# Two expert passes of a routed layer: one loop over both passes, rows copied ahead, and an accumulating scatter into the output

## What is computed

```python
rh = relu(f @ router_w1 + router_b1)              # f = layernorm(x2)
top_w, top_i = top_k(softmax(rh @ router_w2 + router_b2), 2)
w = softmax(top_w)
h1 = relu(f @ expert_w1 + expert_b1)              # 6 experts, 256 x 256 each
h2 = relu(h1 @ expert_w2 + expert_b2)
out = x2 + sum over the two chosen e of w[e] * (h2 @ expert_w3 + expert_b3)[e]
```

## Time and profile before

| | us |
|---|---|
| median of three runs | 787.16 |
| the profiled execution, its own time | 785.95 |
| its span, first to last instruction | 783.9 |
| TensorE busy (matmul) | 677.8 |
| VectorE busy | 556.7 |
| ScalarE busy | 440.9 |
| GpSimd busy | 403.3 |

### The profile page before, as it was taken

The page is one execution under the profiler, slowest core; times in us unless marked ns, Lnnn a source line. Parts: engine busy times, 40 slices in busy tenths (PEclk is TensorE's granted clock), DMA queues, the critical chain, the costliest instruction groups (busy, mean ns, idle before and its releaser), DMA issues.

```text
span 783.9 us, 15402 instructions
## 1 busy us (share of the span) xinstructions
PE 677.8 (86%) x4705; PEld 621.5 (79%) x4705; DVE 556.7 (71%) x1423; ACT 440.9 (56%) x878; POOL 403.3 (51%) x446
## 2 busy tenths in 40 slices
PE   3877999999999888888860899999994799999992
PEld 2867788888888777777750799999993799999992
DVE  5674679888888867777864377777773477777772
ACT  2645566667777446767740465565651565656551
POOL 3465378876666100464444155556554155565553
PEclk9999999999999999989855699999998899999997
DMA  8885644544443454765144524444433534544420
GB/s 220 194 163 125 152 128 132 143 132 119 122 138 107 139 164 156 246 192 180 53 112 118 165 82 139 142 133 135 141 111 103 154 93 130 149 133 147 134 65 29
DMA packets 72463, 106.24 MB, mean 136 GB/s; under 512 B 24612, under 2 KB 45605, under 8 KB 72386
## 3 DMA queue, kind: packets, MB, share of 16 engines
q1 hardware_dynamic: 51074, 72.57, 32.9%
q0 software_dynamic: 21312, 32.69, 13.7%
HBM read 60.32 MB, written 46.78 MB: 137 GB/s over the span
## 4 chain that ended last, share of the span: by engine, by line
PE 74%; DVE 10%; DMA 4%; ACT 3%; issue 3%; POOL 2%; SPq 1%; POOLq 0%; DVEq 0%; ACTq 0%
PE kv_ps L1348 11%; PE kv_ps L1350 10%; PE kv_ps L1349 10%; PE pt L1340 6%; PE d_ps L1212 5%; PE kv_ps L1189 5%; PE kv_ps L1192 4%; PE kv_ps L1190 4%; PE xt_ps L1340 3%; PE kv_ps L1289 2%; PE pt L1189 2%; PE pt L1192 2%; PE pt L1190 2%; POOL tab L571 1%; PE pt L1280 1%
## 5 line engine op out<-in xcount | busy, mean ns | idle before, releaser
L1348 PE MATMUL kv_ps<-we_h,now_h 128*128 x648 | 194.2, 300 | 11.0 <-DVE now_l L1159 4.8
L1350 PE MATMUL kv_ps<-we_h,now_l 128*128 x648 | 185.2, 286 | 0.0
L1349 PE MATMUL kv_ps<-we_l,now_h 128*128 x648 | 185.1, 286 | 0.0
L1348 PEld LDWEIGHTS kv_ps<-we_h,now_h 128*128 128x128 f32 x648 | 125.7, 194 | 15.7 <-issue 15.7
L1349 PEld LDWEIGHTS kv_ps<-we_l,now_h 128*128 128x128 f32 x648 | 125.8, 194 | 0.0
L1350 PEld LDWEIGHTS kv_ps<-we_h,now_l 128*128 128x128 f32 x648 | 125.5, 194 | 0.0
L1137 DVE TENSOR_TENSOR work<-kv_ps,be 128x256 f32<-128x256 f32 x216 | 81.7, 420 | 61.0 <-PE kv_ps L1350 60.7
L582 POOL TENSOR_TENSOR arena<-work,arena 128x256 f32<-128x256 f32 x80 | 53.3, 686 | 105.2 <-ACT work L768 105.2
L775 ACT ACTIVATE now_h<-pt 128x512 fp32r<-128x512 f32 x54 | 32.2, 597 | 112.3 <-PE pt L1340 112.3
L539 POOL DMA_INDIRECT alg<-al_tab,src_all x50 | 62.2, 1244 | 40.1 <-issue 25.9
L947 DVE TENSOR_REDUCE ss<-xring 125x16 f32<-125x1040 f32 x50 | 61.7, 1234 | 17.3 <-ACT xring L653 16.3
(11 more groups left out here) (239 smaller groups left out, 1833.5 us busy)
## 6 DMA issues: line engine op xcount, KB each, us to landing
arena<-tab SPq DMA_DIRECT2D x40, 259.0 KB, 3.0
xring<-in_x SPq DMA_DIRECT2D x26, 224.0 KB
xt_tab<-arena SPq DMA_DIRECT2D x10, 568.8 KB
arena<-tab SPq DMA_DIRECT2D x40, 131.0 KB, 2.1
we_h<-wt_h SPq DMA_DIRECT2D x6, 768.0 KB, 5.5
we_l<-wt_l SPq DMA_DIRECT2D x6, 768.0 KB, 7.7
weight_in<-tab SPq DMA_DIRECT2D x14, 259.0 KB, 3.0
xring<-in_x SPq DMA_DIRECT2D x5, 560.0 KB
```

What stands on the lines that cost most here:

```text
L1348: pe.matmul(outp, hi[:, c, :], we_h[:, w], start=c == 0, stop=False)
L1349: pe.matmul(outp, hi[:, c, :], we_l[:, w], start=False, stop=False)
L1350: last = pe.matmul(outp, lo[:, c, :], we_h[:, w], start=False, stop=c == KC - 1)
```

## The change

One loop of 57 steps runs over all 54 pairs (n = 0 to 53) of both passes, on every engine. `tab1` gets the old rows, 262 numbers, copied straight from the loaded buffer by GpSimd (`second_rows`), eight pairs ahead (`AHEAD`). Pass 0 puts x2 plus the first weighted result into the output by a plain scatter; pass 1 scatters only the second weighted result, and the transfer adds it to what lies in the output (`compute_op=ALU.add`). The sums are built in four buffers of their own, `yw`. In pass 0 VectorE computes row plus weight times bias (`weighted`); in pass 1 ScalarE makes the scaled bias row as before, and nothing adds x2. GpSimd adds nothing more. Pair buffers are smaller and 14 instead of 7. Register loads take two numbers in every step, into one of four sets. Steps of TensorE and the other lines of ScalarE and VectorE keep their order.

```diff
--- before.py
+++ after.py
@@ -45,12 +45,15 @@
-U = 7
-U1 = 5
-EL = 3
+U = 14
+U1 = 10
+EL, SETS = 1, 4
-ROW1 = D + ROW
+ALL = 2 * PAIRS
+AHEAD = 8
+YB = 4
+CB = 6
...
-        tab1 = nc.dram_tensor("tab1", (E * REG + S, ROW1), FP32, kind="Internal").ap()
+        tab1 = nc.dram_tensor("tab1", (E * REG + S, ROW), FP32, kind="Internal").ap()
...
-        rb = [(arena, weight_in)[u >= U1][:, at:at + HB * ROW1].rearrange("p (b n) -> p b n", b=HB)
-              for u in range(U) for at in (u % U1 * HB * ROW1,)]
+        rb = [rows[:, u * HB * ROW:(u + 1) * HB * ROW].rearrange("p (b n) -> p b n", b=HB)
+              for rows, count in ((arena, U1), (weight_in, U - U1)) for u in range(count)]
...
-        b3w = [rows_of(work, HB * F * (2 + b)) for b in range(2)]
+        yw = [rows_of(work, HB * F * (2 + b)) for b in range(YB)]
...
-        def experts(engine, regs, k, j):
-
-            part = regs[(j // EL) % 2]
+        def experts(engine, regs, n):
+
+            k, j = n // PAIRS, n % PAIRS
+            part = regs[(n // EL) % SETS]
+            if j == 0:
+                engine.wait_ge(e_done, k + 1)
             engine.load(part, tab_e[0:1, k, j * HB:(j + EL) * HB])
             return [engine.snap(reg, min_val=0, max_val=E - 1) for reg in part]
...
-            return [[engine.alloc_register(f"{name}{h}_{i}") for i in range(EL * HB)] for h in range(2)]
-
-        def tiles(engine, k, regs, step):
+            return [[engine.alloc_register(f"{name}{h}_{i}") for i in range(EL * HB)] for h in range(SETS)]
...
+        def added(n):
+
+            return z_out[n % YB], 16 * HB * (n // YB + 1)
+
+        def copied(n):
+
+            return second_out[n % CB], 16 * HB * (n // CB + 1)
...
+            for n in range(ALL):
+                k, j = n // PAIRS, n % PAIRS
+                if n == PAIRS:
+                    sp.wait_ge(tab_done, 2)
                 for h in range(HB):
                     first = sp.value_load(tab_row[0:1, k, j * HB + h:j * HB + h + 1], min_val=0, max_val=E * REG)
+                    if h == 0 and n >= U:
+                        sp.wait_ge(*added(n - U))
+                        if n - U < PAIRS:
+                            sp.wait_ge(*copied(n - U))
+                    if n == PAIRS and h == 0:
+                        sp.wait_ge(fill_out[1], 16 * (E + 1))
+                        for m in range(PAIRS - CB, PAIRS):
+                            sp.wait_ge(*copied(m))
+                    sp.dma_start(rb[n % U][:, h, :], (tab0, tab1)[k][bass.ds(first, S), :]).then_inc(r_in[n % U], 16)
+                if n == U - 1:
+                    fill_up(1)
+            for n in range(ALL - YB, ALL):
+                sp.wait_ge(*added(n))
...
+            def second_rows(n):
+
+                u = n % U
+                pool.wait_ge(r_in[u], 16 * HB * (turn(n) + 1))
+                if n >= CB:
+                    pool.wait_ge(*copied(n - CB))
+                for h in range(HB):
+                    pool.indirect_dma_start(
+                        out=tab1, out_offset=bass.IndirectOffsetOnAxis(
+                            ap=rb[u][:, h, C_POS:C_POS + 1].bitcast(I32), axis=0),
+                        in_=rb[u][:, h, :], in_offset=None, bounds_check=E * REG - 1, oob_is_err=False
+                    ).then_inc(second_out[n % CB], 16)
+
+            def put_rows(n):
+
+                u = n % U
+                for h in range(HB):
+                    pool.wait_ge(y_done, n * HB + h + 1)
+                    token = bass.IndirectOffsetOnAxis(ap=rb[u][:, h, C_TOK:C_TOK + 1].bitcast(I32), axis=0)
+                    if n < PAIRS:
+                        pool.indirect_dma_start(out=out, out_offset=token, in_=yw[n % YB][:, h, :], in_offset=None,
+                                                bounds_check=N - 1, oob_is_err=False).then_inc(z_out[n % YB], 16)
+                    else:
+                        pool.indirect_dma_start(out=out, out_offset=token, in_=yw[n % YB][:, h, :], in_offset=None,
+                                                bounds_check=N - 1, oob_is_err=False, compute_op=ALU.add).then_inc(z_out[n % YB], 16)
+
+            for n in range(AHEAD):
+                second_rows(n)
+            for n in range(ALL):
+                if n == PAIRS:
+                    for m in range(PAIRS - YB, PAIRS):
+                        pool.wait_ge(*added(m))
+                put_rows(n)
+                if n + AHEAD < PAIRS:
+                    second_rows(n + AHEAD)
...
+            def third_bias(n, es):
+
+                act.wait_ge(*added(n - YB))
+                for h in range(HB):
+                    w = C_W + n // PAIRS
+                    act.activation(yw[n % YB][:, h, :], b3_sb[:, bass.ds(es[n, h] * D, D)], ACT.Copy,
+                                   scale=rb[n % U][:, h, w:w + 1]).then_inc(b3w_ready, 1)
...
+                if has(n) and n >= PAIRS:
+                    third_bias(n, es)
+
+            normal(0)
+            tiles(act, act_e, step)
...
+            def weighted(n, es):
+
+                if n < PAIRS:
+                    if n >= YB:
+                        dve.wait_ge(*added(n - YB))
                     for h in range(HB):
+                        row = rb[n % U][:, h, :]
+                        dve.scalar_tensor_tensor(yw[n % YB][:, h, :], b3_sb[:, bass.ds(es[n, h] * D, D)], row[:, C_W:C_W + 1], row[:, 0:D],
+                                                 ALU.mult, ALU.add).then_inc(xb_done, 1)
+                    dve.wait_ge(xb_done, (n + 1) * HB)
+                else:
+                    dve.wait_ge(b3w_ready, (n - PAIRS + 1) * HB)
+                dve.wait_ge(l3_done, n + 1)
+                for h in range(HB):
+                    w = C_W + n // PAIRS
+                    dve.scalar_tensor_tensor(yw[n % YB][:, h, :], l3_ps[n % 2][:, h, :], rb[n % U][:, h, w:w + 1], yw[n % YB][:, h, :],
+                                             ALU.mult, ALU.add).then_inc(y_done, 1)
...
+            tiles(dve, dve_e, step)
```

More of the change, by code:

```diff
@@ L572, in _ @@
                                             in_=xr[g % RB][:, j, :], in_offset=None).then_inc(sc_out[g % RB], 16)
[L575 to L593, removed]
-                            ).then_inc(z_out[u], 16)
-                        else:
-                            pool.indirect_dma_start(
-                                out=out, out_offset=bass.IndirectOffsetOnAxis(
-                                    ap=rb[u][:, h, D + C_TOK:D + C_TOK + 1].bitcast(I32), axis=0),
-                                in_=rb[u][:, h, 0:D], in_offset=None, bounds_check=N - 1, oob_is_err=False
-                            ).then_inc(z_out[u], 16)
-                for j in range(PAIRS + 2):
-                    if has(j):
-                        third_bias(j)
-                    if has(j - 2):
-                        scatter(j - 2)
@@ new lines, in step @@
+            def step(n, es):
+                if has(n):
+                    dve.wait_ge(l1_done, n + 1)
+                    plus_bias(hs1, l1_ps, 0, n, es, hs1_done)
+                if has(n - 1):
+                    dve.wait_ge(l2_done, n)
+                    plus_bias(hs2, l2_ps, 1, n - 1, es, hs2_done)
+                if has(n + 1):
+                    dve.wait_ge(in_h_done, n + 2)
+                    dve.tensor_tensor(in_l, tin_ps, in_h.bitcast(FP32), ALU.subtract).then_inc(in_l_done, 1)
+                if has(n):
+                    dve.wait_ge(h1_h_done, n + 1)
+                    dve.scalar_tensor_tensor(h1_l, th1_ps, 0.0, h1_h.bitcast(FP32), ALU.max, ALU.subtract).then_inc(h1_l_done, 1)
+                if has(n - 2):
+                    weighted(n - 2, es)
+                if has(n - 1):
+                    dve.wait_ge(h2_h_done, n)
+                    dve.scalar_tensor_tensor(h2_l, th2_ps, 0.0, h2_h.bitcast(FP32), ALU.max, ALU.subtract).then_inc(h2_l_done, 1)
@@ new lines, in step @@
+            def step(n, es):
+                if has(n):
+                    pe.wait_ge(in_l_done, n + 1)
+                    for h in range(HB):
+                        last = expert_layer(l1_ps[:, h, :], 0, in_h[:, h, :, :], in_l[:, h, :, :], es[n, h])
+                    last.then_inc(l1_done, 1)
+                if has(n - 1):
+                    pe.wait_ge(h1_l_done, n)
+                    for h in range(HB):
+                        last = expert_layer(l2_ps[:, h, :], 1, h1_h[:, h, :, :], h1_l[:, h, :, :], es[n - 1, h])
+                    last.then_inc(l2_done, 1)
+                if has(n + 1):
+                    pe.wait_ge(xe_done, (n + 2) * HB)
+                    turned(tin_ps, xe[:, (n + 1) % 2, :, :]).then_inc(tin_done, 1)
+                if has(n):
+                    pe.wait_ge(hs1_done, (n + 1) * HB)
+                    turned(th1_ps, hs1).then_inc(th1_done, 1)
+                if has(n - 2):
+                    m = n - 2
+                    pe.wait_ge(h2_l_done, m + 1)
+                    if m >= 2:
```

(8 more changed lines are left out.)

175 lines of the change are left out of this document (39 added, 136 removed).

## The result

The changed kernel takes **757.06 us** (median of 4 runs, 755.16 to 760.47) where the kernel before takes 786.73 on the same chip (784.31 to 787.74): a ratio of 0.963, 95% interval 0.961 to 0.966. The forecast was 762.0: the way was right, and the time lies 1.9 us under the range's lower end of 759. The profiled execution took 760.47. There is a second result that the forecast did not have at all: kernels of this form ran on six occasions, and on three of them all but one took 807 to 822 us; the unaltered changed kernel, which ran on two of these three, took 815 and 809 us.

A forecast was written before the change was run, and what follows sets the result against it. The prediction took TensorE to set the pace in both passes, with a hole at the pass change. From 785.95 us it took 25.1 off (hole 19.76, register loads 5.33) and added 0.5: 761.4, said as 762; range 759 to 771.

The forecast's parts named there:

- The pass change: Between pass 0 and pass 1: one loop closes the hole where TensorE runs dry, 19.76 us less.
- the loads: TensorE's six-number register loads in both passes: short loads in every step cause no stall, 5.33 us less.
- The place where `tab1` could have been late: At the boundary, the load of pair 27 after the last copies: three steps, 17 us, against a load's 3.17; no wait.
- The price of a two-number load: Register loads in every step: some 380 ns each, at most 893, under the 1202 that TensorE's queue hid.
- The slack: VectorE in pass 0: 1.23 us of slack hides two new bias instructions of 0.93 us per pair; at worst 5 us.
- Rival A: VectorE is late in pass 0 by 0.3 to 0.5 us per pair: 770 to 775 us; chance 0.12.
- Accumulating scatters: Pass 1's adding scatters into the output: landing in 4 to 7 us, at worst 10, hidden unless it takes 9.
- Rival B: Accumulating scatters pace pass 1 if one takes over 2.8 us; kernel slower, 826 us at 4.0 each; chance 0.06.
- The end: After the last scatter, GpSimd's closing drain: a slower landing costs nothing to 3 us, taken as 0.5 us more.
- The sum: Whole kernel: profiled execution 785.95 us, less 25.1, plus 0.5, gives 761.4 us.
- The 7% given to "slower": Whole kernel: chance 0.07 of being slower, from accumulating scatters pacing pass 1 (0.06) or short loads stalling TensorE (0.01).

## Why the prediction was right and where it was wrong

**The pass change and the loads: right.** Forecast 19.76 + 5.33 = 25.1 us, measured 25.3, with the parts confirmed by the kernels that make one change alone (for the loads 5.2 inside the steps of the kernel before, 4.5 in the merged loop). The place where `tab1` could have been late was not late: step 26 to step 29 are 5.61 us each.

**Loads.** The price of a two-number load was put at 380 ns, from a line between 275 and 816; it is 536, and 947 at most. The step that carried the term was that TensorE's queue hides up to 1.2 us of a load, and 947 is under that. A wrong price and a right bound. The bound is sharper than the forecast knew: pass 0 lost its 3.03 us not in four equal parts but in five steps, 0.19 us beside a load of 1397 ns, 0.28 beside 1480, 0.82 beside 2027 and 0.84 beside each of two of 2047; pass 1 lost 0.42 to 0.70 beside loads of 1624 to 1857 ns. In all nine a load cost what it had over 1.16 to 1.21 us.

**VectorE: right, and too cautious.** 0.87 us against 0.88 forecast. The slack was put at 1.23 us against 0.93, with 0.2 to spare; it holds another 0.43. Rival A is out. Of the 0.81 us that lay between the adds of `hs1` and their transposes, 0.53 are left (542.74 to 543.27). Nor do the new instructions wait for GpSimd's scatters:

```profile
L1146 DVE SCALAR_TENSOR_TENSOR work<-xring,arena x40: 474/479/534, 455.5 to 585.0; 128x256 f32<-128x256 f32 x40
```

534 ns at most in a stretch where scatters are made in over half of the time: by the rule of the Trainium skill (SBUF — State Buffer, Who interferes with whom) each could have waited for one, if making a scatter's descriptors counted as reading SBUF. The trace shows no such wait, as the forecast took it.

**Accumulating scatters: right in effect.** Landing was put at 4 to 7 us and is 3.8 at the median, just under, and 1.6 times the plain one. The Trainium skill (Collectives: The Full Stack, The bandwidth ceiling) says half the rate; the trace shows less than a doubling of the landing. What the sum had no term for is the cost in GpSimd itself, 1.55 us instead of 0.98. Rival B's limit was 2.8, so it holds by a wide margin: 2 x 1.85 = 3.7 of 5.61 us.

**The end: wrong, and this failed the range.** The step was "a slower landing costs nothing if that drain is a fixed time, up to 3 us if it begins when the scatter lands. I take 0.5": bounds of 0 and +3, none below nothing. Measured: -2.7. It is the sum of three terms, none of them forecast. The closing row of six scatters begins 8.87 us after step 52's transposes instead of 766.97 - 756.45 = 10.52, so 1.65 less; GpSimd's adds are gone, and with them put back it is 2.0 more. The six take 10.81 us instead of 7.80, so 3.0 more. And the drain ends 4.91 us after the last of them (753.53 to 758.44) instead of 8.86, so 3.95 less.

The kind of the scatters and the rest of the change do not simply add: the end is 27.45 us before and 27.52 with accumulating scatters, 26.07 in the changed kernel with plain ones and 24.75 with accumulating ones. So the kind is worth nothing in the one and 1.3 us in the other, and the rest of the change 1.4 with plain and 2.8 with accumulating scatters, of which the adds are 2.0. With one program the drain's end moves nearer to the last scatter when the scatters accumulate: 5.84 us behind it instead of 8.86 in the kernel before, 4.91 instead of 7.44 in the changed one. But the kind does not set it alone. Without pass 0's puts the last scatters accumulate too and end as long after step 52 (19.8 us against 19.7), yet the drain ends 7.1 us behind them; with copies three pairs ahead it is 6.0:

```profile
756.30 1.55 POOL L605 DMA_INDIRECT out_x<-work,weight_in  x1 [0.30 <-issue]
...
L80 POOLq DRAIN  x1: 10458/10458/10458, 754.5 to 754.5; - x1
```

So the drain is neither of fixed length (4.07 to 10.90 us were seen) nor one that takes a fixed time from the last scatter. What sets it stays open.

**The rounding.** The sum was 761.4; to come from the profiled execution to the median, 762 was said (the full 1.2 would have made it 762.6). With the right end term the sum is 785.95 - 25.3 - 2.7 = 757.95, which lies among the medians of the quiet occasions, 757.06 to 758.52. The lower end of 759 allowed for no gain in any term, though dropping 108 adds from the last engine to finish is a gain.

**The missing rival.** "It drops 108 adds, and gets four scatters a step in pass 0 instead of two ... No cost" compared GpSimd's time with the step (5.1 of 5.62 us) and asked only whether GpSimd falls behind. Nothing in the trace of before, with two a step, could show what four do to the other engines on a disturbed occasion. But it was a doubling of a kind of traffic that the trace had never held in this stretch, and it had no line in the rivals. The 7% given to "slower" was for other mechanisms.

## What to carry to other kernels

A hole between two passes costs its data's trip through DRAM and about as much again in draining and refilling (9 of 20 us here); running one pipeline through both, with the copies made some eight pairs ahead, removes both. Count the end of the kernel by the engine that finishes it: instructions that this engine loses or gains in a step can show up in the last steps even when the loop hides them (2.0 us here for GpSimd's adds). And where a change doubles the number of indirect DMAs in a stretch, time it on several occasions, with the unaltered kernel on each: the unaltered changed kernel came to a ratio of 0.96 here on three occasions and to 1.03 and 1.04 on two others.

## What the runs showed of the hardware

- An accumulating scatter of 128 rows of 256 numbers took 1.55 us of GpSimd where a plain one took 0.98, and landed in 3.8 us instead of 2.4.
- A two-number register load took 0.53 us on TensorE and VectorE and 0.49 on ScalarE; six numbers took 0.81 to 2.05 on TensorE, and in the kernel before each cost the step what it had over some 1.2 us.
- GpSimd's closing drain took 4.07 us with nothing outstanding, and otherwise ended 4.9 to 8.9 us after the last scatter's end.
- On some occasions, while GpSimd made scatters four a step, TensorE's signals were recorded up to 6.6 us after the matmuls' modelled ends instead of 0.01, and VectorE and ScalarE waited for them for 2 to 7 us; in the stalls read out above they started again together 1.0 to 1.2 us after the row of scatters ended.
